# The scan phase's order by table: one time and one PSUM bank for each job, and Silu calls regrouped

## What is computed

```python
# layer 1, for each of 4 sequences; 512 channels, 16 states, 512 time steps
x  = silu(conv4(in_proj(ctx)) + conv_b)
dt, Bm, Cm = split(x_proj(x));  dt = softplus(dt_proj(dt) + dt_b)
state = state * exp(dt * A) + (dt * x) * Bm      # step by step over time
y  = (sum over states of state * Cm) + D * x
x1 = x_in + swap(y * silu(layernorm(x_in)))
# layer 2, h = layernorm(x1)
scores = softmax(h @ gate_w.T); top 6 of 64 experts
moe    = sum over the 6 of score * (silu(h @ Wg[e]) * (h @ Wu[e])) @ Wd[e]
shared = (silu(h @ sw_gate) * (h @ sw_up)) @ sw_down
out    = x1 + moe + shared
```

## Time and profile before

| | |
|---|---|
| median of 3 runs | 1169.33 us (1167.05 to 1171.11) |
| the profiled execution | 1168.47 us, its span 1166.7 us |
| scan 0 starts, scan 127 starts | 57.2 us, 705.2 us |
| the four batches, from first scan to first scan | 141.8, 171.1, 175.7, 159.4 us |
| from the start of scan 127 to 760 us | 55 us: the last batch's routing |
| from 760 us to the end | 407 us: expert phase |
| busy over the span | PE 79%, DVE 51%, POOL 51%, ACT 41% |

### The profile page before, as it was taken

The page is one execution under the profiler, slowest core; times in us unless marked ns, Lnnn a source line. Parts: engine busy times, 40 slices in busy tenths (PEclk is TensorE's granted clock), DMA queues, the critical chain, the costliest instruction groups (busy, mean ns, idle before and its releaser), DMA issues.

```text
span 1166.7 us, 12225 instructions
## 1 busy us (share of the span) xinstructions
PE 922.5 (79%) x4049; PEld 502.5 (43%) x4049; DVE 590.3 (51%) x833; ACT 477.9 (41%) x853; POOL 590.1 (51%) x334
## 2 busy tenths in 40 slices
PE   5446636567889767889769995899999899997966
PEld 2144335454344454344455445444444443443432
DVE  2087977959657859667859754321212112111111
ACT  3556653765572765472765512322121212111111
POOL 0498799966497856487857650112121211122211
PEclk9568765668989857999969996899999999998988
DMA  9332434432322533323433628399999999999992
GB/s 322 110 126 73 145 110 145 145 120 83 111 86 95 178 134 108 110 78 104 144 114 137 226 99 318 146 340 394 395 401 390 400 399 391 392 390 401 384 318 28
DMA packets 68361, 250.50 MB, mean 215 GB/s; under 512 B 10522, under 2 KB 13094, under 8 KB 68044
## 3 DMA queue, kind: packets, MB, share of 16 engines
q1 hardware_dynamic: 56332, 226.14, 51.2%
q0 software_dynamic: 7744, 18.88, 6.6%
q10 hardware_dynamic: 4224, 4.72, 1.2%
HBM read 230.54 MB, written 19.17 MB: 214 GB/s over the span
## 4 chain that ended last, share of the span: by engine, by line
PE 45%; DMA 15%; DVE 13%; ACT 9%; issue 9%; POOL 8%; SPq 1%; POOLq 0%; DVEq 0%; ACTq 0%
PE ps L697 10%; PE ps L567 9%; PE ps L734 9%; DMA out_rows<-xn,idxs 5%; DMA arena<-xn_rows,idu 5%; PE ps L758 4%; POOL arena L1342 3%; PE ps L710 3%; DVE ps L1106 3%; DVE arena L1106 3%; DMA arena<-bc_rows 3%; DVE arena L1113 2%; POOL arena L1347 2%; PE ps L778 2%; ACT ps L919 2%
## 5 line engine op out<-in xcount | busy, mean ns | idle before, releaser
L567 PE MATMUL ps<-ident,arena 128*128 128x128 f32 (+2 forms) x1408 | 252.6, 336 | 153.2 <-POOL arena L1347 91.5
L567 PEld LDWEIGHTS ps<-ident,arena 128*128 128x128 f32 (+2 forms) x1408 | 215.8, 186 | 257.6 <-POOL arena L1347 105.3
L1342 POOL TENSOR_TENSOR arena<-arena 128x1024 f32<-128x1024 f32 x128 | 299.7, 2355 | 27.4 <-PE ps L567 15.0
L919 ACT ACTIVATE ps<-arena,An 128x511 f32<-128x511 f32 x256 | 165.8, 680 | 195.1 <-DVE ps L1114 150.9
L1106 DVE TENSOR_TENSOR_SCAN ps<-ps,arena 128x1024 f32<-128x1024 f32 x76 | 174.0, 2289 | 48.9 <-ACT ps L919 36.5
L1366 POOL DMA_INDIRECT out_rows<-xn,idxs x32 | 50.9, 1592 | 279.1 <-ACT xn L818 151.5
L1347 POOL TENSOR_TENSOR arena<-arena 128x1024 f32<-128x1024 f32 x52 | 122.3, 2352 | 117.1 <-DVE arena L1106 117.1
L697 PE MATMUL ps<-xnT,sw 128*128 128x512 f32 (+1 forms) x328 | 160.2, 629 | 8.7 <-ACT hs L818 8.7
L734 PE MATMUL ps<-arena 128*64 128x352 f32 x968 | 165.8, 480 | 0.0
L1106 DVE TENSOR_TENSOR_SCAN arena<-ps,arena 128x1024 f32<-128x1024 f32 x52 | 118.9, 2286 | 31.7 <-POOL arena L1342 29.0
L1246 DVE TENSOR_TENSOR arena<-arena,ps 128x352 f32<-128x352 f32 x32 | 16.7, 521 | 208.0 <-PE ps L734 208.0
(11 more groups left out here) (150 smaller groups left out, 936.4 us busy)
## 6 DMA issues: line engine op xcount, KB each, us to landing
arena<-bc_rows SPq DMA_DIRECT2D x128, 512.0 KB, 4.6
arena<-in_L_ffn_w_down SPq DMA_DIRECT2D x60, 768.0 KB, 20.5
arena<-in_L_ffn_w_gate SPq DMA_DIRECT2D x61, 704.0 KB, 20.6
arena<-in_L_ffn_w_up SPq DMA_DIRECT2D x60, 704.0 KB, 18.1
arena<-in_x SPq DMA_DIRECT2D x4, 1024.0 KB, 6.8
xn_rows<-xn ACTq DMA_DIRECT2D x4, 1024.0 KB, 4.5
out_rows<-arena SPq DMA_DIRECT2D x4, 1024.0 KB, 4.9
extra<-in_L_ffn_w_up SPq DMA_DIRECT2D x4, 704.0 KB
```

Source lines behind the costliest of these rows:

```text
L567: return nc.tensor.matmul(dst, src, ident[0:k, 0:k], is_transpose=True, **kw)
L919: a = nc.scalar.activation(ps[:, 2 * (c % 2) + n, 1:L], dt[k][:, 1:L], ACT.Exp, scale=An[:, k, NB * g + n:NB * g + n + 1])
L1342: G.tensor_tensor(R[c % RING], dtu[k][:, None, :].to_broadcast([P, NB, L]), Brep[n % REPS], ALU.mult)\
```

## The change

The formulas and `grab` are gone. Two tables, `AT` for every batch and `LAST` for the jobs of the last one that differ, give each job its time relative to the first step of its batch; `BANKS` and `LASTBANKS` give its bank; `STEP` the offsets of a step's own jobs. All batches now have the same order, with the last one's differences. `EXTRA` names five even steps of a batch that VectorE weighs (4, 6, 12, 22, 24) in place of three (6, 14, 22). What is loaded and multiplied is the same; only order, banks and the owner of those `weigh` jobs differ.

```diff
+AT = {
+    "act u": [-24.06, -22.26, -20.32, -20.29],
+    "dve conv": [-24.45, -24.0, -23.05, -22.29],
+    "dve table": [52.32],
+    "act ssilu": [56.45, 59.37, 59.38, 59.39, 59.67, 61.0],
...
+STEP = {
+    "dbu": -2.13,
+    "dA": -1.19,
+    "weigh": 0.22,
...
+EXTRA = [4, 6, 12, 22, 24]
...
         def by_vector(q):
-            return q % 2 == 1 or q % STEPS in (6, 14, 22)
+            return q % 2 == 1 or q % STEPS in EXTRA
...
             for q in range(NQ):
                 b, k, g = step_of(q)
-                add(q - 1.8, "pool", "dbu", b, q)
-                add(q - 1.3, "act", "dA", b, q)
+                add(q + STEP["dbu"], "pool", "dbu", b, q)
+                add(q + STEP["dA"], "act", "dA", b, q)
                 add(q, "dve", "scan", b, q)
...
+                for job in sorted(set(AT) | set(LAST)):
+                    engine, kind = job.split()
...
+                    times = LAST.get(job, AT.get(job)) if b == B - 1 else AT[job]
+                    banks = LASTBANKS.get(kind, BANKS.get(kind)) if b == B - 1 else BANKS.get(kind)
...
+                        add(STEPS * b + t, engine, kind, b + XBS if kind == "x_load" else b, c)
```

More of the change, by code:

```diff
@@ new lines @@
+BANKS = {
+    "ctx": [7, 6],
+    "inproj": [6, 7, 6, 7],
+    "xdbl": [6],
+    "dt": [7, 6, 7, 6],
+    "zT": [6, 6, 7, 6],
+    "xnT": [7, 6, 6, 6],
+    "logits": [7],
+    "sgate": [6, 6, 7, 6, 7, 6],
+    "pos": [7],
+    "table": [7],
+    "sup": [6, 7, 6, 7, 6, 7],
+    "sdown": [6, 7, 6, 7],
+}
+LASTBANKS = {
+    "xnT": [1, 2, 6, 0],
+    "logits": [3],
+    "sgate": [0, 1, 0, 1, 0],
+    "pos": [2],
+    "table": [1],
+    "sel": [1],
+}
+STEP = {
+    "dbu": -2.13,
+    "dA": -1.19,
+    "weigh": 0.22,
+    "yT": 1.4,
+    "yTp": 1.43,
+    "duT": 0.64,
+    "gate": 1.77,
+    "x2": 2.12,
+    "rep": -5.13,
+}
@@ L46, in build @@
+EXTRA = [4, 6, 12, 22, 24]
+EACH = ['acc', 'c', 'conv', 'ctx', 'dt', 'dtu', 'du', 'exp', 'inproj', 'ln', 'logits', 'ohsid', 'scopy', 'score', 'sdown', 'sgate', 'shs', 'sp', 'ssilu', 'sup', 'u', 'xdt', 'xn', 'xnT', 'xstats', 'zT', 'zs', 'zstats']
 def build(nc, x, ctx_1024, in_proj_w, conv_w, conv_b, x_proj_w, dt_proj_w, dt_proj_b, A_log, D,
@@ L250, in first_phase @@
+            last_only, not_last = ("sel", "ids"), ("sup", "shs", "ssilu", "sdown")
             for b in range(B):
[L251 to L259 removed]
```

266 lines of the change are left out of this document (105 added, 161 removed).

## The result

The changed kernel takes 1084.12 us (median of 4 runs, 1081.06 to 1084.48); the kernel before, run on the same chip between them, 1170.22 (4 runs, 1167.05 to 1172.09). The profiled execution took 1084.39 us, its span 1082.5.

The account below looks back on a forecast made before the run. It took VectorE's waits, set by order, as what bounds a scan phase with no full engine in batches 1 to 3, the expert phase following one for one. Terms: −17−22−24−14+12+8−2+9+6 = −44, giving 1125 us, range 1095 to 1163.

Parts of the forecast that it names:

- TensorE's own load: Batches 1 to 3: TensorE's busy time leaves little room, so 3 us added for each: +9 us.
- Routing: Batches 0 to 2: waits of `top` and `choose` fall from 29.2 us to 12, 4 a batch: −17 us.
- Preparation: Next batch's preparation, `conv` eight steps earlier: waits for `dA` fall from 36.5 us to 14: −22 us.
- Shared up: Shared expert's `sup` products: `shs` waits fall from 38.9 us to 15, 5 a batch: −24 us.
- sdown: Shared expert's `sdown`, spread out or behind the scans: waits fall from 17.6 us to 3: −14 us.
- table: `table` directly behind scan 84 waits 3.9 to 5.2 us for its last product: +12 us for three batches.
- weigh moved: Two `weigh` jobs a batch go from GpSimd to VectorE: +8 us in batches 1 to 3, −2 in batch 0.
- Silu groups: 18 more table loads on ScalarE, 23 us, taken as covered by other work: nothing booked beyond scan 77's 1.8 us.
- The rival that put the groups on the `dA` chain: Slower rival: Silu group visits delay the `dA` behind them, other gains partly lost: 1200 us; chance of slower 0.12.
- End: After the last scan: `sdown` products make it 12.5 us later, warm TensorE and a half `sgate` give some back: +6 us.
- smaller waits still: Rival: TensorE at full clock through routing, waits of 1 us there and 2 at `shs`: 1098 us; chance 0.14.
- TensorE as the bound: Rival: products, not order, set `shs` and `sdown` waits, and half the preparation's gain stays out: 1160 us; chance 0.15.

Follow-up runs that it names:

- lean_after: Changed kernel without half of the shared expert's products of batches 0 to 2: 1070.5 us.
- e_tableb: Changed kernel with VectorE's copy of the table one step later (53.3 for 52.32): 1084.1 us.
- e_tbank: Changed kernel with VectorE's copy of the table two steps later and `sgate` product groups in other banks, clear of the table's: 1085.0 us.
- u_extra: Changed kernel with the three old even steps weighed by VectorE (6, 14, 22) in place of the five new ones: 1098.7 us.
- u_silu: Changed kernel with the Silu calls in one group of `u` and one of `ssilu` for each batch, 18 table loads fewer: 1086.3 us.
- u_scalar: Changed kernel with the old offset of `dA` alone (1.3 steps ahead of its scan for 1.19): 1109.5 us.
- u_scalaru: Changed kernel with the old `dA` offset (1.3), but the third and fourth `u` calls of a batch put together again: 1092.2 us.
- lean_before: Kernel before without half of the shared expert's products of batches 0 to 2: 1118.1 us.
- u_step: Changed kernel with all offsets of a step's own jobs as in the kernel before: 1131.3 us.
- a_prepfirst: Kernel before with the next batch's preparation taking its PSUM banks ahead of layernorm and routing, nothing else: 1169.1 us.
- a_pstepx: Kernel before with preparation ahead of routing, the new step offsets and the five even steps weighed by VectorE: 1136.6 us.
- u_weigh: Changed kernel with the old offsets of the weighting (0.6 for 0.22), the gate and the x half alone: 1092.2 us.
- e_early: Changed kernel with batch 2's shared expert earlier in batch 3, other `sgate` banks and its six `ssilu` calls in one group: 1085.3 us.

## Why the prediction was wrong

It named the right direction and the right idle engine; the size was off by half. Three steps of it failed, each answered below: the surcharge for TensorE's own load and for half clock (+9, and a part of the −17), the price of the moved `weigh` jobs (+8 and −2, measured −15), and the step offsets, which had no term and are worth 47 us in this order. What it gave as signs came true for the waits (`choose` under 1 us, `shs` under 20, no scan 7 us late, the wait before `table`) and not for the lengths of the batches, which were all below it, nor for the end (15.0 us to the first transpose for 12). By its own steps:

*What bounds the kernel*: right. VectorE's work is the same and its idle time went, the expert phase kept its length, and lean_after excludes TensorE's load as the bound.

*Routing* left 4 us a batch: measured 0.9 in all, a term of −28 for −17. The estimate was the middle between full and half clock, and at these places the full-clock value was the right one: in the 8 us ahead of `top` the granted clock is 1.00 in all three batches.

*Preparation* left 14: measured 9.4 for scans behind `dA`, and `conv` lost its 6.4 as well, −33 for −22. *Shared up* left 15, measured 10.7: −28 for −24. *sdown* left 3, measured 6.7: −11 for −14. *table*: 10.7 for 12, three waits of up to 4.3 us as foretold. But e_tableb and e_tbank show that these 10.7 are no cost: the term +12 was a correct wait and a wrong price.

*weigh moved*, +8 and −2: wrong sign. u_extra gives −15. The step took VectorE, the fuller engine, as the bound of those batches, although the same text had it idle for 44 us a batch; what counts instead, probably how soon the bank pair and the buffer come free, no run singles out. It is no property of the edit: in the old order it costs 5.

*Silu groups*, 0: right for the groups as they are (u_silu, without the 18 loads, is 2 us slower). The loads have a price all the same, where they stand between two `dA`: 17 us for six loads and one changed pair in u_scalar. The rival that put the groups on the `dA` chain described a mechanism that exists and that the changed kernel just avoids. The Trainium skill's page "ScalarE: Activation LUTs" says in its Rules for kernel authors to do all work of one set before switching; u_silu and u_scalaru show both sides, nothing gained where the load is covered and 17 us where it is not. Of the drain for each switch that the same page gives (What ACT_TABLE_LOAD costs) the trace shows nothing: 110.90+1.28 is 112.18, and `dA` starts at 112.19.

*TensorE's own load*, +9, and the half-clock share in the routing term: this step was wrong as reasoning, whatever the other terms did. The walk through the new order had given 149 us for a middle batch at full clock; batches 1 and 2 took 142.6 and 148.2. I put a surcharge on it, from the granted clock and the busy time of the *old* order. The clock was 0.79 and 0.85 there and is 0.85 and 0.93 in the new one, with nearly the same products in shorter batches. That the lost waits raised it is likely and not shown alone: lean_before has fewer waits and fewer products, and its clock in these batches is 0.75 and 0.80. As to the load, lean_after leaves half of the shared expert's products out and gains 1.6 and 1.7 us in batches 1 and 2.

*Batches 0 and 3* were not walked. I booked −2 for batch 0, it gained 10.8; u_step takes back all of it, u_extra alone 6.0, so neither part does it by itself. Batch 3 was put near 145 us, 14 less; it is 131.0, 28.4 less and as much as the others gained.

*The step offsets* had no term: 47 us if taken back, 17 of them through one pair of calls that the table fits to the new offset, and 41 if put alone into the old order. The walk of one batch held them without my knowing, and I gave the credit to the moved jobs. a_prepfirst shows that moving preparation and routing by itself gives nothing. The 41, the 31 of a_pstepx and the 15 of u_extra depend on each other and can't be added up to the 86.

*End*, +6: it was +11.4. The products ran 20.4 us for 19.6 and began 8.1 us behind scan 127, for the 6.3 that the earlier trace rows had let me expect: the first transpose comes 15.0 us later, not 12.5. The full clock gave back 4.3 for 4. The 2 us for the half `sgate` ahead of `pos` did not come: from `top` to the first expert product it is 30.3 us for 29.8. From `top` to `pos` it is 3.1 us less (2.5 for 5.6), but the half group only moved behind `pos`, where TensorE now has ten products ahead of the table for eight (8.75 us for 7.03), and the last eight now wait 0.9 us for the ids and run at a granted clock of 0.71 for 0.81 (9.99 us for 8.83).

Of the rivals, smaller waits still (1098) came nearest, though 1084 is just below its own range (1085 to 1108) too. Of its reasons, full clock in the routing and nothing of the 9 came true, and `shs` waited 3.6 us a batch for its 2. It knew nothing of the offsets either. TensorE as the bound is excluded, and so is the slower case for this kernel.

**What stays open**: which queue carries the 41 us of the offsets in the old order; which chain bounds the steps around the table, that is, what makes `shs`'s products and `dbu` as late as they are when the copy no longer waits; and whether the last routing's 11 us can be had back.

## What to carry to other kernels

Where in-order queues run side by side, first look at the rows that belong together in every step: here their offsets were worth 41 to 47 us, in either order. A row that frees a buffer is a candidate for the place right behind the one that fills it, ahead of anything that may wait (in the changed kernel that place is worth up to 8 us, u_weigh). When a walk of the new order with measured durations gives a number, walk every kind of stretch and keep the number; a surcharge from the old kernel's clock or idle time may count what the change removes. And before moving a row because it waits, ask whose buffer it holds, and whether the wait is on the path at all: here 10.7 us of waiting were free, and avoiding them carelessly cost 15.

## What the hardware showed beside

A load of an activation table is 1.28 us wherever it stands, and the next call starts behind it within 0.01 us; its price went from none that shows (u_silu, 18 loads fewer and 2.2 us slower) to 2.9 (u_scalar against u_scalaru, 17 us for six loads, with the chain behind them). After 20.42 us of products without a gap the last batch's transposes and router products took 6.20 us at a granted clock of 1.00, and after a pause of TensorE of 6.3 us in e_early, like the 7.1 us in the earlier trace rows, eight transposes took 1.96 us instead of 1.23, at a granted clock of 0.50.
